# First attention layer: row maxima half a batch later, merged and moved VectorE operations, another order of the side work

## What is computed

```python
x = x + _L0_xattn_ref(_layernorm(x), ctx_1024, ctx_1024)
...
q = Q.reshape(B, S, 16, 16).transpose(0, 2, 1, 3)      # k, v likewise
scores = jnp.einsum('bhqd,bhkd->bhqk', q, k) * scale
attn = jax.nn.softmax(scores, axis=-1)
out = jnp.einsum('bhqk,bhkd->bhqd', attn, v)
...
logits = flat @ gate_w + gate_b                        # flat: _layernorm(x) of the next layer
```

## Time and profile before

| | |
|---|---|
| median of three runs | 1271.04 us (1270.32 to 1271.66) |
| profiled execution | 1270.46 us, span 1268.7 us |
| TensorE busy | 1136.6 us, 90% |
| VectorE busy | 932.5 us, 73% |
| ScalarE busy | 742.0 us, 58% |
| GpSimd busy | 589.3 us, 46% |

### The profile page before, as it was taken

How to read it: one execution, slowest core, us unless ns; L and a number is a source line. 1 busy time by engine, 2 the same in 40 slices (tenths; PEclk the granted TensorE clock), 3 DMA queues, 4 the chain that set the end, 5 groups by cost and what they waited for, 6 DMA issues and landing times. The chain is left out here.

```text
span 1268.7 us, 26854 instructions
## 1 busy us (share of the span) xinstructions
PE 1136.6 (90%) x9615; PEld 929.3 (73%) x9616; DVE 932.5 (73%) x1378; ACT 742.0 (58%) x978; POOL 589.3 (46%) x555
## 2 busy tenths in 40 slices
PE   3789999979879999999999999927899999999997
PEld 2456666549869999999999999815666666668886
DVE  7898999729448887888877877558888888853332
ACT  3477777856445565464555555333777777764443
POOL 1377677344458588652203000067877776201221
PEclk9999999988989999999999999955999999999999
DMA  5656666429954645562213111055566665511221
GB/s 191 209 186 234 234 218 210 144 85 328 335 184 127 196 153 170 168 203 76 73 50 107 41 50 41 26 188 197 190 212 209 203 201 191 181 44 51 75 73 44
DMA packets 120983, 193.41 MB, mean 152 GB/s; under 512 B 12160, under 2 KB 64384, under 8 KB 120768
## 3 DMA queue, kind: packets, MB, share of 16 engines
q1 hardware_dynamic: 95840, 140.71, 32.6%
q0 software_dynamic: 12576, 39.07, 10.1%
q10 hardware_dynamic: 12480, 12.47, 2.9%
HBM read 91.80 MB, written 49.55 MB: 111 GB/s over the span
## 5 line engine op out<-in xcount | busy, mean ns | idle before, releaser
L2153 PE MATMUL y_ps<-e_w,hiddenT_hi 128*128 x624 | 225.1, 403 | 1.8 <-DVE slot_y L2257 1.8
L2189 ACT ACTIVATE hidden<-hidden 128x1024 f32<-128x1024 f32 x78 | 82.8, 1062 | 183.3 <-DVE hidden L2222 182.8
L2136 PE MATMUL h_ps<-slot_xT_hi,tile_w_hi 128*128 128x256 f32 x624 | 177.7, 285 | 3.2 <-DVE slot_xT_lo L2240 3.2
L2136 PE MATMUL h_ps<-slot_xT_lo,tile_w_hi 128*128 128x256 f32 x624 | 177.2, 284 | 0.0
L2136 PE MATMUL h_ps<-slot_xT_hi,tile_w_lo 128*128 128x256 f32 x624 | 177.2, 284 | 0.0
L1476 DVE TENSOR_REDUCE neg_max<-big 128x4 fp32r<-128x1024 f32 x128 | 154.6, 1222 | 29.6 <-PE big L1223 24.4
L2154 PE MATMUL y_ps<-e_w,hiddenT_lo 128*128 x624 | 175.1, 281 | 0.0
L603 DVE TENSOR_REDUCE neg_max<-big 128x4 fp32r<-128x1024 f32 x128 | 155.2, 1222 | 17.1 <-PE big L404 14.6
L535 ACT ACTIVATE probs<-big 128x1024 f32<-128x1024 f32 x128 | 131.0, 1023 | 55.1 <-PE big L415 54.1
L1383 ACT ACTIVATE probs<-big 128x1024 f32<-128x1024 f32 x128 | 130.8, 1023 | 39.5 <-PE big L1234 35.9
L2246 DVE TENSOR_TENSOR hiddenT_lo<-hidden,hiddenT_hi 128x1024 fp32r<-128x1024 f32 x78 | 98.7, 1306 | 58.2 <-ACT hiddenT_hi L2200 53.7
(11 more groups left out here) (238 smaller groups left out, 2587.3 us busy)
## 6 DMA issues: line engine op xcount, KB each, us to landing
k_stack<-k_cut SPq DMA_DIRECT2D x96, 256.0 KB, 2.5
q_stack<-q_cut SPq DMA_DIRECT2D x96, 256.0 KB, 3.0
e_w<-in_L_ffn_w POOLq DMA_DIRECT2D x10, 1024.0 KB, 6.8
slots_out<-slot_y ACTq DMA_DIRECT2D x39, 256.0 KB
slots_in<-staging POOLq DMA_DIRECT2D x38, 256.0 KB
slot_x<-slots_in SPq DMA_DIRECT2D x38, 256.0 KB
vals<-in_v_wide SPq DMA_DIRECT2D x16, 512.0 KB, 4.1
v_wide<-v_out SPq DMA_DIRECT2D x16, 512.0 KB, 5.3
```

The lines of the kernel that those rows point to most:

```text
L2136: last = nc.tensor.matmul(h_ps[k][:, f % HF, :], w1[w][b.u][:, c, f * P:(f + 1) * P], xT[a][b.u][:, c, :], start=(n == 0), stop=(n == 3 * ...
L2153: nc.tensor.matmul(y_ps[q][:].rearrange("p s d -> p (s d)"), hT[0][o.u][:, f, rows], both, start=(f == 0), stop=False)
L2189: nc.scalar.activation(half(hidden, k), half(hidden, k), ACT.Gelu).then_inc(gelu_done, 1)
```

## The change

1. The maxima of a batch are made half a batch later: slots 4 to 7 of body b make pairs 0 to 3 of batch b + 2, slots 0 to 3 of body b + 1 pairs 4 to 7 (`maxima`).
2. The output rows of a batch are transposed in one go in slot 2, into a buffer of the ring `big`, with one reciprocal and one multiplication on VectorE instead of two.
3. Variance plus epsilon moves from VectorE to GpSimd (`power`).
4. `turn_q` and both q copies move from slot 1 to 6, VectorE's low part to slot 7; the logits to slot 1 of the next body (one more body at the end); `turn_neg` to slot 4; the statistics of x to slots 4 and 5.
5. SyncE issues the norm store and the load of v first and the negated maxima ahead of k's stack; GpSimd adds the residual before the power of the next x.

```diff
+    LN_STEPS = 2 * QT
+    OUT_AT = 2
+    HALF = PAIRS // 2
+    def maxima(b, g):
+        return divmod((b + 1) * PAIRS + g + HALF, PAIRS)
...
         for g in range(PAIRS):
-            big_order += [(name, t) for name, t in ((("max", g), b + 2), (("score", g), b)) if has(t)]
+            m, gm = maxima(b, g)
+            big_order += [(name, t) for name, t in ((("max", gm), m), (("score", g), b), ("out" if g == OUT_AT else None, b - 1))
+                          if has(t) and name]
...
-            def power(veps, rs, ln_done, rs_ready, t):
+            def power(mv, veps, rs, ln_done, rs_ready, t):
                 pool.wait_ge(ln_done, (t + 1) * LN_STEPS)
+                nc.gpsimd.tensor_scalar(veps[:], mv[:, :, 1], EPS, None, ALU.add).then_inc(rs_ready, 1)
+                pool.wait_ge(rs_ready, 2 * t + 1)
                 nc.gpsimd.tensor_tensor(rs[:], veps[:], neg_half[:, 0:QT], ALU.pow).then_inc(rs_ready, 1)
...
-            def out_rows(d, q):
+            def out_rows(d):
                 for gg in range(GROUPS):
                     read_spare(pe, (("pv", gg), d))
-                bank = free_spare(pe, (("out", q), d))
-                for gg in range(GROUPS):
-                    last = nc.tensor.transpose(spare[bank][:, gg * P:(gg + 1) * P], outT[d % 2][:, gg, q * P:(q + 1) * P], ident[:])
-                last.then_inc(filled[bank], 1)
+                bank = free_big(pe, ("out", d))
+                for q in range(QT):
+                    for gg in range(GROUPS):
+                        last = nc.tensor.transpose(big[bank][:, q, gg // 2, gg % 2 * P:(gg % 2 + 1) * P], outT[d % 2][:, gg, q * P:(q + 1) * P], ident[:])
+                last.then_inc(big_filled[bank], 1)
...
-            def out_rows(d, q):
-                bank = full_spare(dve, (("out", q), d))
+            def out_rows(d):
+                bank = full_big(dve, ("out", d))
...
-                nc.vector.reciprocal(recip[:, q, :], heads[:, :, DH]).then_inc(recip_done, 1)
-                dve.wait_ge(recip_done, d * QT + q + 1)
+                nc.vector.reciprocal(recip[:], heads[:, :, :, DH]).then_inc(recip_done, 1)
+                dve.wait_ge(recip_done, d + 1)
```

More of the change, by code:

```diff
@@ L374, in body @@
                     split_k(b + 3)
+                if has(b - 1):
+                    residual(b - 1)
                 if has(b + 4):
-                    power(var_eps, rstd, ln_step, rstd_ready, b + 4)
+                    power(mean_var, var_eps, rstd, ln_step, rstd_ready, b + 4)
                 if has(b + 4) and b + 4 >= RAMP:
@@ L381, in body @@
                 if has(b - 1):
-                    residual(b - 1)
                     if has(b - 3):
@@ L478, in body @@
                 for g in range(PAIRS):
-                    if has(b + 2):
-                        row_max(b + 2, g)
+                    m, gm = maxima(b, g)
+                    if has(m):
+                        row_max(m, gm)
                     if has(b):
@@ L499, in body @@
                     elif g == 4:
+                        if has(b + 1):
+                            turn_neg(b + 1)
                         if has(b - 2):
@@ L505, in body @@
                     elif g == 6:
-                        if has(b - 2):
-                            logits(b - 2)
+                        if has(b + 3):
+                            turn_q(b + 3)
                     elif g == 7:
@@ L561, in body @@
             def body(b):
-                if has(b + 4) and b + 4 < 4:
-                    clear_k(b + 4)
-                if has(b + 3) and b + 3 < RAMP:
-                    k_hi_out(b + 3)
                 if b == 3:
@@ L576, in body @@
                 for g in range(PAIRS):
+                    if g == HALF and has(b + 4) and b + 4 < 4:
+                        clear_k(b + 4)
+                    if g == HALF and has(b + 3) and b + 3 < RAMP:
+                        k_hi_out(b + 3)
                     if has(b):
@@ L655, in body @@
             def body(b):
[L656 to L659 removed]
                 for g in range(PAIRS):
[L661 to L663 removed]
+                    if g == HALF and has(b + 4) and b + 4 < 4:
+                        nc.vector.memset(q_stack[b + 4][:], 0.0).then_inc(q_zeroed, 1)
+                    if g == HALF and has(b + 3) and b + 3 < RAMP:
+                        k_lo_out(b + 3)
+                    m, gm = maxima(b, g)
+                    if has(m):
+                        reduce(m, gm)
+                    if g == 0:
+                        if has(b + 3) and b + 3 < RAMP:
+                            apply(b + 3)
+                    elif g == 2:
+                        if has(b - 3):
+                            logits(b - 3)
+                        if has(b - 1):
+                            out_rows(b - 1)
+                    elif g == 4:
                         if has(b + 4):
```

89 lines of the change are left out of this document (32 added, 57 removed).

## The result

The changed kernel takes **1268.83 us** (median of 20 runs, 1264.83 to 1275.57) against 1276.14 (20 runs in the same rounds, 1270.32 to 1284.23): ratio **0.994, 95% interval 0.9925 to 0.9954**, 7 us faster. The forecast was no change, 1271.5 against 1271.04. The 1268.83 lies inside the stated range of 1266.0 to 1277.5, but by luck of the rounds: the kernel before took 1276.14 in the same ones, 5 more than in the runs that the forecast started from. The profiled run took 1268.89 us, its span is 1267.1.

A forecast was written before the change was run, and what follows sets the result against it. VectorE and TensorE, neither plainly the limit, were taken as tied by a ring of three buffers; first-stage terms -4.6 - 1.6 - 5.05 + 7.7 + 3.3 + 0.75 gave +0.5 on 1271.04, so 1271.5 us, range 1266.0 to 1277.5.

The forecast's parts named there:

- ramp: Before the first score: 12 reductions stand there instead of 16, -4.6 us.
- bodies 0 to 2: First three bodies of the first stage: 0.55 us less for each, -1.6 (bounds 0 and -3).
- bodies 3 to 11: Nine bodies at 14.1 us each, 126.9 instead of 131.95: -5.05 (bounds -7 and 0).
- body 12: ScalarE waits for the late w2 load: shift 6.8 us, then 2.9 for TensorE at half clock, +7.7.
- bodies 13 to 15: Maxima moved in +1.7, TensorE hold-up in body 13 +0.5, second w2 half 1.4 late +1.1: +3.3 us.
- tail: End of the first stage: division waits for all eight transposes, residual for both rows, +0.75 us.
- Steady body: Repeating body of the first stage: 14.1 us against 14.4, VectorE waiting for TensorE ahead of slots 0, 1 and 2.
- GpSimd at 0: The epsilon adds moved to GpSimd cost 0 in its free 4.7 us a body, 0.1 in the tail.
- the load was neither cheap: Rival, body 12: the late w2 load is cheap, no clock fall or a shift of 5; 1267.6 us, chance 0.21.
- the ring at 14.4: Rival, steady body: TensorE's full slots and eight transposes hold VectorE at period 14.4; 1274.8 us, chance 0.25.
- q's transfers at slot 4: Rival, steady body: q's low part issued late, its transfer holds slot 4 of the next body; 1282 us, chance 0.05.
- VectorE alone: Rival, steady body: VectorE is the only bound, 12.8 us a body; 1255 us, chance 0.05.

The follow-up runs named there:

- experiment 4: The changed kernel with the two additions of epsilon per body put back on VectorE: 1274.31 us, 0.9987 of the kernel before.
- experiment 6: The kernel before with only the additions of epsilon moved from VectorE to GpSimd: 1277.02 us, 1.0004 of the kernel before.
- experiment 10: Second profiles of both kernels, nothing edited: the changed kernel 1269.66 us (0.9942 of the kernel before), the kernel before 1271.6 us in one run.
- experiment 1: The changed kernel with ScalarE's copies of w2 halves in bodies 12 and 14 moved from slot 0 to slot 4: 1261.58 us, 0.9885 of the kernel before.
- experiments 1 to 3: The changed kernel with w2 copies in mid-body (1261.58 us), the first w2 load 2.5 us earlier (1269.05), or repeated matmuls in TensorE's gap (1269.01 narrow, 1269.11 wide).
- `fill_gap`: The changed kernel with the 8-column logits matmuls in slot 1 of body 12 issued six times: 1269.01 us, body 12 20.93.
- `fill_long2`: The changed kernel with the 256-column score matmuls in slot 1 of body 12 issued 27 times: one profiled run, body 12 20.37 us.

## Why the prediction was wrong

The whole time moved by -0.6% where no change was forecast; the stage by -6.6 where +0.5 was summed. Term by term, from the first profile of each kernel:

| term | forecast | measured |
|---|---|---|
| ramp | -4.6 | -4.6 |
| bodies 0 to 2 | -1.6 | -3.6 |
| bodies 3 to 11 | -5.05 | -7.3 |
| body 12 | +7.7 | +6.25 |
| bodies 13 to 15 | +3.3 | +1.5 |
| tail | +0.75 | +1.1 |

The mechanisms were right, but for the wait on the second half of w2, which costs nothing. The step that failed is the sum: four of its terms were mis-sized, and all four came out lower than forecast, by 2.0 (bodies 0 to 2), 2.3 (bodies 3 to 11), 1.45 (body 12) and 1.8 (bodies 13 to 15).

- **Ramp**: right in size. First maximum of body 0 at 38.60, forecast 38.65. Within it two things that were left out nearly cancel: the first reduction comes 0.37 later (18.93 for 18.56), and the stretch from there is 4.97 shorter, not 4.56.
- **Steady body**: 13.84, not 14.1; 2.3 over nine bodies. The waits came as worked out: slots 0, 1 and 2 start 1.66 apart where 1.68 and 1.67 were forecast, slot 3 follows 2.26 later as forecast. What was wrong is VectorE's work in slots 5 and 6, of which "two aggregates 0.27" was read from rows in which an add waited for them; measured without the add: 0.16. From slot 5 to 7 the forecast had 2.07 and 1.41, the trace has 1.91 and 1.28. The same rows mis-priced the adds, "0.37 and 0.17 at least": experiment 4 gives 0.19 each, and experiment 6 shows that the 0.37 hid a wait for ScalarE. The 14.1 was built from the rows that remain, so the price of the adds doesn't enter it; the aggregates and the shorter statistics (0.63 for 0.69 in slot 5) do, with 0.16 in slot 5 and 0.13 in slot 6, and they make up the difference.
- **Bodies 0 to 2**: forecast 0.55 less for each. Bodies 1 and 2 gave 0.6 to 0.7 each; body 0 gave 2.15 in the first pair of profiles and 1.90 in the second, and the three together -3.6 and -3.2 (42.66 against 45.90). The step that failed is to price body 0 like the later ones: it starts with matmuls at half rate (experiment 10), for 6.4 us in the change and 10.4 before (12.3 and 15.1 in the second pair), which the forecast did not look at. At half rate at most half of a stretch is lost, so 4.0 and 2.8 us less of it can give up to 2.0 and 1.4 (an estimate), where 1.4 and 1.2 are missing; no run tested it.
- **Body 12**: the added wait that the diff doesn't show was there, with its place, its releaser (a DMA), its length (6.56, forecast 6 to 8) and the half clock behind it. Shift 6.1 for 6.8: the load is issued 2.37 behind the body's first maximum where 2.7 was taken, and exp 0 ends at 8.6 where 9.2 was. Half clock 1.8 to 2.1 for 2.9: from the maxima of slot 2 to those of slot 4 TensorE takes 6.16 (212.74 to 218.90) instead of the steady body's 3.49 (123.84 to 127.33), 2.7 more, and some 0.6 of that is made up by the end of the body. The base of 13.8 that the forecast put under both has no working in it, beside its own period of 14.1; that it fits the measured 13.84 is luck.
- **Bodies 13 to 15**: the second half of w2 was to be "1.4 late (+1.1)"; ScalarE stands 0.87 for it, but with that copy in mid-body (experiment 1) the three bodies take 36.7 instead of 36.44, so the term is nothing. Of the 0.5 of hold-up by TensorE in body 13, 0.26 is there (slots 0 to 4 take 6.88 instead of 6.62). The last 0.4 of the 1.8 isn't settled.
- **Tail**: +1.1 for +0.75; what the other 0.35 is wasn't looked into.
- **GpSimd at 0**: right. In the steady body it still stands 2.88 ahead of its add, for VectorE's aggregates (after, GpSimd's timeline):

```profile
145.04 0.23 POOL L340 TENSOR_SCALAR var_eps<-mean_var 128x2 f32<-128x2 f32 x1 [2.88 <-DVE mean_var L627]
```

- **Rivals**: the load was neither cheap (experiments 1 to 3) nor was the ring at 14.4, TensorE did not wait for q's transfers at slot 4 of the steady body, and VectorE alone (12.8 a body) was not the bound.

A lower bound had been set for each of the four: bodies 0 to 2 -3, the nine bodies -7, body 12 a shift of 5, bodies 13 to 15 +1.5. The first two were passed by 0.6 and 0.3, the last one was met. But the chances counted the downward side only through the rivals (0.26), not through several terms that come out low together.

## What to carry to other kernels

Before costing an instruction that is taken away, look at what waits for the one ahead of it: what a neighbour costs from start to start changes with the wait behind it (0.27 and 0.16 here), and the removed one's own row may hold a wait for another engine (0.37 for 0.08 here). A saving counts only in the order that can use it (the same adds were worth 0 before and 0.30 a body after), and a large term with a plus sign in a forecast, here the late load, is first a thing to repair: one block moved to where its data has landed doubled the gain. Read mechanisms from the length of a body in the trace, and the whole time from many runs.

## What the runs showed of the hardware that was not expected

- The granted clock fell to 0.50 at about 211.3 with TensorE busy 1.00 of every microsecond, in matmuls of 8 columns (`fill_gap`), and stayed at 1.00 with matmuls of 256 columns in the same place (`fill_long2`). The Trainium skill (TensorE: Matmul & The Clock Gate, section on what is actually happening) says that a hardware block sets the gate by how busy the array has been recently. Behind the empty gaps of 5.77 and 3.63 the trace agrees; in `fill_gap` the profile's busy share gave no sign of the fall.
- Up to about 45 us, or 50.7 in the second profile, four maxima matmuls take 0.80 and pv 1.93, against 0.50 and 1.07 later, while the granted clock of those windows is recorded as 1.00:

```profile
46.00:48.00 2.00, 2.00 (x16) 1.28 (x18) 2.00 (x4) 1.45 (x3) 0.00 (x0) 1.00 0.01 4
```

  Sixteen matmuls in 2 us here, in the second profile of the change, against 27, 30 and 34 in the three windows of 48 to 54 in the first. In the ramp the durations tell the rate and the column does not.
- Two aggregates of 6 elements take 0.16 from start to start when the next VectorE work needs nothing of them, 0.27 when it waits for them.
